# Relation scores: the gather engine waits for the store of the raw source rows itself, not for ACT's word behind its tile moves

## What is computed

```python
h_proj = jnp.einsum('nd,rde->rne', h, relation_weight)      # 32 relations
t_r = h_proj[etype, src]
h_r = h_proj[etype, dst]
att = jnp.sum(t_r * jnp.tanh(h_r + efeat), axis=-1)         # one score per edge
...                                                         # softmax over the edges of a node
msg = h[src] * a[:, None]                                   # needs h[src] again, later
```

## Time and profile before

| | |
|---|---|
| median of 3 timed executions | 10767.73 us (10759.51 to 10779.53) |
| profiled execution | 10839.79 us, span 10838.1 us |
| the stage `relation_scores` | from 494 to 2724 us of the span |
| POOL over the span | 4149.2 us busy, 38% |
| PE, DVE, ACT over the span | 39%, 42%, 21% busy |

### The profile page before, as it was taken

The page is one execution under the profiler, slowest core; times in us unless marked ns, Lnnn a source line. Parts: engine busy times, 40 slices in busy tenths (PEclk is TensorE's granted clock), DMA queues, the critical chain, the costliest instruction groups (busy, mean ns, idle before and its releaser), DMA issues. The chain is left out here.

```text
span 10838.1 us, 92266 instructions
## 1 busy us (share of the span) xinstructions
PE 4214.8 (39%) x26157; PEld 3240.1 (30%) x26157; DVE 4577.5 (42%) x7317; ACT 2322.6 (21%) x3572; POOL 4149.2 (38%) x4401
## 2 busy tenths in 40 slices
PE   1300000000025551444444255454557555444466
PEld 1100000000015551444444223232347333332266
DVE  6522222222831112433443244444477444444577
ACT  0011111111310000443433233333310133333300
POOL 0377777676010003444344334444410244444210
PEclk9655555555558885676766567777779577777797
DMA  3433333333436663222222211211135121211153
GB/s 144 178 84 88 95 85 88 92 97 84 162 76 223 224 224 102 66 72 70 71 90 66 30 46 45 47 48 44 46 74 116 30 50 45 47 46 46 31 124 64
DMA packets 996837, 937.20 MB, mean 86 GB/s; under 512 B 856274, under 2 KB 857422, under 8 KB 986657
## 3 DMA queue, kind: packets, MB, share of 16 engines
q1 hardware_dynamic: 425264, 588.81, 16.2%
q0 software_dynamic: 141536, 217.12, 9.3%
q10 hardware_dynamic: 429960, 130.45, 4.9%
HBM read 654.37 MB, written 281.43 MB: 86 GB/s over the span
## 5 line engine op out<-in xcount | busy, mean ns | idle before, releaser
L419 POOL DMA_INDIRECT both<-table,stage_i x2352 | 2223.0, 945 | 791.7 <-issue 728.3
L1910 DVE TENSOR_TENSOR lz<-psZ,att 128x650 f32<-128x650 f32 x784 | 650.4, 830 | 1695.7 <-ACT psZ L1874 1291.0
L1827 PE MATMUL psZ<-wrl,bothT 128*128 128x325 f32 x3136 | 1335.8, 518 | 0.0
L1826 PE MATMUL psZ<-brl,ones 128*128 128x325 bf16 x1568 | 546.6, 349 | 1559.3 <-ACT bothT L1864 798.7
L465 PE MATMUL psA<-hot 128*128 128x125 bf16 x1425 | 166.0, 308 | 2065.7 <-remote 749.1
L419 POOL DMA_INDIRECT rows_s<-hpx,stS x784 | 806.5, 1029 | 267.8 <-issue 257.4
L1874 ACT ACTIVATE psZ<-psZ 128x640 f32<-128x640 f32 x784 | 541.4, 691 | 1684.4 <-PE psZ L1827 684.3
L419 POOL DMA_INDIRECT rows_d<-hpx,stD x784 | 749.1, 956 | 252.4 <-issue 250.8
L416 POOL COPY stage_i<-srcI 128x28 int32 x84 | 17.1, 204 | 2033.7 <-ACTq L1868 735.6
L465 PEld LDWEIGHTS psA<-hot 128*128 128x128 bf16 x1425 | 137.6, 141 | 2094.1 <-issue 1478.0
L1826 PEld LDWEIGHTS psZ<-brl,ones 128*128 128x128 bf16 x1568 | 169.8, 108 | 1768.8 <-ACT bothT L1864 886.7
(11 more groups left out here) (407 smaller groups left out, 8443.7 us busy)
## 6 DMA issues: line engine op xcount, KB each, us to landing
tile<-adj SPq DMA_DIRECT2D x228, 781.2 KB, 4.5
xs<-x_src SPq DMA_DIRECT2D x648, 128.0 KB
starts<-start_rows SPq DMA_DIRECT2D x84, 896.0 KB, 4.5
hpx<-stage SPq DMA_DIRECT2D x25, 2048.0 KB, 7.3
ea<-in_ea SPq DMA_DIRECT2D x28, 1792.0 KB
x_src<-both ACTq DMA_DIRECT2D x56, 896.0 KB
adj<-tile SPq DMA_DIRECT2D x57, 781.2 KB
both<-table,stage_i POOLq DMA_INDIRECT x2352
```

The source lines that it names most:

```text
L419: pool.indirect_dma_start(buf[:, k, j, 0:width] if width == buf.shape[3] else buf[:, k, j, D:2 * D], None, table, bass.IndirectOffsetOnAxi ...
L1826: pe.matmul(psZ[:, q % 2, j, 0:HD + H], g.ones3[:, :], g.brl3[:, :], start=True, stop=False)
L1827: last = pe.matmul(psZ[:, q % 2, j, 0:HD + H], bothT[:, q % 2, j, :], g.wrl[:, :, :].rearrange("k h c -> k (h c)"), start=False, stop=True)
L1910: v.tensor_tensor(lz[:, n % 4], psZ[:, n % 2, :, 0:HD + H], g.att1[:, :, :].rearrange("p h c -> p (h c)").unsqueeze(1).to_broadcast([P, G, ...
```

## The change

ACT no longer waits for its store and no longer counts `kept`. POOL waits on `stored[k]` itself, the semaphore that the store's DMA raises by 16. ACT starts both `stored` semaphores with 16, so that the first chunk of each buffer passes, and waits once for both behind its loop. Two semaphores go.

```diff
-        used, kept = [s.sem(f"used{k}") for k in range(2)], [s.sem(f"kept{k}") for k in range(2)]
+        used = [s.sem(f"used{k}") for k in range(2)]
...
                         pool.wait_ge(used[k], i + 1)
-                        pool.wait_ge(kept[k], i + 1)
+                        pool.wait_ge(stored[k], i * 16 + 16)
                         gather_columns(pool, g.hpx, 2 * D, g.hpS, stS, rows_s, c, i, k, got_s, staged)
...
                 for k in range(2):
-                    act.sem_inc(kept[k], 1)
+                    act.sem_inc(stored[k], 16)
                 tiles.act_begin(act)
...
                             tiles.move(act, i * TB + r, r % 2, i * (TB // 2) + r // 2)
-                        act.wait_ge(stored[k], i * 16 + 16)
-                        act.sem_inc(kept[k], 1)
+                for k in range(2):
+                    act.wait_ge(stored[k], (NCH // 2) * 16 + 16)
                 tiles.move(act, NT - 1, 0, NT // 2)
```

## The result

The changed kernel takes 10821.1 us (median of 7, 10804.35 to 10846.03), the kernel before 10761.87 (7 timings): ratio 1.0051, 95% interval 1.0042 to 1.0061. It is 59 us slower. The range held. The case on which it was centred, no change (0.54), did not come; rival 2 (0.26), the wait that moves to `used`, did.

What follows compares the result with a forecast made beforehand. POOL was taken to bound the stage, with 121.1 us of waits for `kept`. On the median, lateness everywhere (+44 and +22, +66) gave 10834, no net change 10768, all waits gone 10647; forecast 10768, range 10705 to 10828.

Steps and rivals of the forecast that it cites:

- rival 2: Heads of POOL's chunks: the wait moves to `used` and becomes longer, +40 to +66 us, 10808 to 10834; chance 0.26.
- What bounds the stage: POOL's gathers bound the 2230 us stage; its nine waits for ACT's `kept`, 121.1 us, are the most to win.
- What is late: Counts of PE's matmuls reach ACT's moves late, 70 us a tile, either in every execution or only because of recording.
- the 72 us: Profiled execution's excess over the median, 72.06 us: a sign that recording causes the lateness.
- The 49 us: Profiled execution without its nine waits is 10718.7; the median, 49 us above, speaks against recording being the whole cause.
- The step from recorded to timed executions: Recording can throttle an engine; by this alone timed executions have no waits and the change gives 0 us.
- The wait moves to `used`: POOL would stop at chunks 5, 10, 15, 20 and 25, waiting for `used` instead of `kept`, if lateness is real.
- Its length, 33 us: Each POOL wait on `used`: ready at 373, 12.3 us of silence, then 20 us to `used`, starting at 406.
- POOL's sum, +44: Five POOL waits of 33 us, 165 us, where there were 121.1 us: +44 us.
- The tail, +22 us: Stage end after POOL's last gather: 12.3 us of silence and about 12 from count to add instead of 1.8.
- Rival 3: One more chunk of slack absorbs lateness with late tiles of 37 to 55 us: 10707 or 10647; chance 0.20.
- rival 1: Nothing measurable, within 0.2%: timed executions rarely wait for `kept`, or stalls removed and added nearly cancel; 10768, chance 0.54.

Runs made afterwards that it cites:

- store-alone run: Kernel before, with POOL waiting for the raw-row store itself and ACT's `kept` still behind the tile moves: 10759.44 us, ratio 0.9998 to before.
- the long rows: Changed kernel, ACT copying raw rows and storing 128 rows of 7168 bytes instead of 3584 of 256: ratio 0.9997 (8682.78 us); on another chip 1.0082 (10914.77 us).
- the store twice: Changed kernel, with the store of the raw rows issued a second time into its own scratch: 8685.08 us, ratio 0.9999 to before.
- one wait in four: Changed kernel, with POOL's wait for the tile moves put back at one chunk in four: 10759.46 us, ratio 0.9994 to before.
- half-tile kernels: Kernel before and changed kernel, each with 13 matmuls to a tile instead of 25: 10742.54 us (ratio 0.9981) and 10750.44 us (0.9983).

## Why the prediction was right and where it was wrong

- *What bounds the stage, and that POOL waits for the moves and not for the store*: right, by the run with the store alone.
- *What is late: in all executions or only in the recorded one.* This is the step that failed. I read the 72 us between the profiled execution and the median as a sign that timed executions may be free of the lateness, and gave "nothing measurable" 0.54. The store-alone run shows the nine waits in an execution of 10763.9 us of span. A large part of the 72 us lay elsewhere: the group in the last layer was idle for 52 us more in that execution than in the profiled one after (1643.8) and in the store-alone run (1643.4). The 49 us that I held against the reading was the stronger number: even if all 72 us had been late counts, 49 of the 121.1 would have been left in a timed execution. I gave it too little weight. The step from recorded to timed executions, by which the timed ones would have no waits and the change would give 0 us, failed with it: the timed ones are 59 us longer.
- *The range*: it held 10821.1, but it was laid around 10768 for a case that did not come, and its upper end cut off a part of rival 2. That the outcome fell inside is in part luck.
- *The wait moves to `used`, once in five chunks, at 5, 10, 15, 20, 25*: right to the chunk, on two chips.
- *Its length, 33 us*: 32.3, 20.2, 34.4, 16.2 and 20.2 in the profile after, 31.3 on the average on the chip at 10828. In the three shorter waits the last tile that `used` hangs on ended 1.0 us behind, 3.2 us before and 2.4 us behind POOL's last gather, so only the chain of some 20 us was left and no silence was needed. The place is right; the length was worked out for the worst case and taken for all five.
- *POOL's sum, +44*: this term failed. The five waits were priced at 165 us and took 123.2, so the move from `kept` to `used` cost 2.1 us instead of 44. What made up +32.1 are the 36.8 us of stalls behind POOL's own index copies, a term that I had at nothing. That the two sums are near each other is luck. On the chip at 10828 both terms are there, some 35 and 41 us.
- *The tail, +22 us*: 8.2 in the profile after, where the last late tile ended at 2735.8, with POOL's last gather, so the 12 us of silence did not come. On the chip at 10828 the silence came (12.9 us from POOL's last gather to the end of the late tile), and the tail grew by 21.3.
- *Rival 2's +40 to +66*: measured +59, made up otherwise than in the working, and +95 on the chip at 10828, which is beyond it by the stalls that the working did not have.
- *A reading*: late moves start 11.2 us apart (1389.22 - 1378.03), not 10.5; that is about the idle time before them. The 70.0 us of a tile stand, and the sum goes by them.
- *Rival 3, faster*: its condition, a late tile under 55 us, isn't met; late tiles take 70.0 us. Where the tile was cut to half its matmuls (six late groups 5.6 us apart, some 35 us a tile), both kernels came out alike, as rival 1 has it for any pace under 37 us. The changed kernel as it is was not timed on a chip of the 8685 kind; there its two relatives, with the long rows and with the store twice, stand at 0.9997 and 0.9999.
- *The removed instructions and the added one*: no cost to be seen; the store-alone run, which has them on POOL as well, is at 0.9998.

**What stays open.** What makes the counts late is not known. It comes with gathers issued for long without a pause, it goes within 12 to 16 us after the last one, it grows with the number of matmuls, it reaches POOL's own counts, it does not hang on the store's packets, and in the stage it is absent on two chips of four. Every timing here comes with a span and a clock, so it seems that no execution was free of recording, and whether the recording makes the lateness can't be told. That the block which writes the event records holds its producers back sooner than lose one (the Trainium skill, NOTIFIC — the notification-queue block, section 7.1) fits the signs, and no run here proves it.

It also stays open whether there is a fixed rate (theory B). From the first head to the last gather a chunk takes 78.9 us before (with (2703.2 - 494.2) / 28), 78.6 in the store-alone kernel and with one wait in four, 78.2 in each of the two half-tile kernels, and 80.0 after, where 74.4 is the rate on the chip at 8685. Whether POOL stops at heads or behind its copies, the sum of the stops is much the same: 121.1, 114.4, 107.3, 129.9 and 125.3 us in the same order. Only the half tiles beat the kernel before beyond the interval, and by 0.2%.

## What to carry to other kernels

A wait that looks like pure loss can be what lets its own releaser catch up: before it is taken away, ask what the chain behind it does while the engine is silent, and which wait comes next if that chain no longer gets the silence. When a chain needs more time for a chunk (140 us here) than the engine in front (74.5), one more chunk of slack only makes the waits rarer and longer: nine of 13.5 us became five of 24.6, or of 31.3 on another chip. And where the silence is gone, look for stalls at other counts of the same engine, which here cost more than the longer waits did. A difference between one profiled execution and a median says nothing of a stage until another profile has shown the stage.

## What was not expected of the hardware

- One program takes 10763, 10828, 8685 or 8681 us depending on the chip, up to 25% apart, at the same instructions. In the six kernels traced on the two chips of the 8685 kind the moves of a tile are never late in this stage. A change that is a 0.5% or 0.9% loss on one kind has no late count to act on there.
- POOL's first gather started up to 7.0 us behind POOL's own 0.2 us copy that it waits for, where 0.8 us is usual; such stalls began some 220 to 260 us into gathers without a pause.
